# Gathers without a bound for their indices, in a transformer block with two edge stages

## What is computed

```python
# GNN, for each of 4 heads
e = e_src[:, src] + e_dst[:, dst]
e = jnp.where(e > 0, e, NEG_SLOPE * e)
m = jax.ops.segment_max(e_h, dst, num_segments=N)
ex = jnp.exp(e_h - m[dst])
den = jax.ops.segment_sum(ex, dst, num_segments=N)
alpha = ex / jnp.maximum(den[dst], 1e-16)
out = jax.ops.segment_sum(alpha[:, None] * z_h[src], dst, num_segments=N)
...
# FFN, the routing over its own edges, then the experts
e = jax.nn.leaky_relu(a_src[src] + a_dst[dst], negative_slope=0.2)
msg = h[src] * alpha[:, :, None]
...
hh = jax.nn.gelu(x @ W1[ei] + b1[ei], approximate=False)
out = out + g[..., None] * (hh @ W2[ei] + b2[ei])
```

## Time and profile before

| | us |
|---|---|
| median of 3 runs | 3594.51 |
| lowest and highest | 3592.44, 3606.05 |
| span of the profiled execution | 3619.3 |
| POOL busy in it | 2173.4 |
| DVE busy in it | 1738.3 |
| PE busy in it | 1464.3 |
| ACT busy in it | 1386.9 |

### The profile page before, as it was taken

One profiled execution on the slowest core, in us unless ns is written; L12 is line 12 of the kernel. 1 busy time (PEld: TensorE's weight loads), 2 busy tenths in 40 slices (PEclk: granted clock), 3 DMA queues, 4 the chain that ended last, 5 costly groups with the idle time before them and its releaser, 6 DMA issues. The chain is left out here.

```text
span 3619.3 us, 23786 instructions
## 1 busy us (share of the span) xinstructions
PE 1464.3 (40%) x4490; PEld 918.6 (25%) x4490; DVE 1738.3 (48%) x3400; ACT 1386.9 (38%) x3540; POOL 2173.4 (60%) x2136
## 2 busy tenths in 40 slices
PE   2556610211212112211514665656665656663014
PEld 1333410111111111111512333433343333332003
DVE  7667786877778777864922111111111111111137
ACT  1332346666776677752402222322222222221112
POOL 0543656666666666645666666666666666666750
PEclk8677855555555555555556777867787777776557
DMA  3421645565666656636521111111111111111166
GB/s 127 130 63 53 170 130 178 199 197 183 199 199 207 192 184 203 196 113 197 149 86 17 33 36 33 38 21 36 36 36 35 33 24 36 35 35 36 17 203 234
DMA packets 227607, 391.61 MB, mean 108 GB/s; under 512 B 53316, under 2 KB 184051, under 8 KB 220113
## 3 DMA queue, kind: packets, MB, share of 16 engines
q1 hardware_dynamic: 137556, 258.07, 20.5%
q0 software_dynamic: 80880, 124.27, 14.9%
q10 hardware_dynamic: 9100, 8.50, 0.7%
HBM read 201.15 MB, written 189.55 MB: 108 GB/s over the span
## 5 line engine op out<-in xcount | busy, mean ns | idle before, releaser
L1229 POOL DMA_INDIRECT stage_got<-ffn_rows,stage_idx x1024 | 1033.8, 1010 | 546.1 <-issue 326.6
L1229 POOL DMA_INDIRECT edges_got<-gnn_rows,edges_idx x728 | 727.9, 1000 | 354.3 <-issue 310.6
L1340 DVE TENSOR_TENSOR_SCAN stage_y<-stage_decays,stage_y 128x960 f32<-128x960 f32 (+2 forms) x288 | 527.1, 1878 | 172.8 <-ACT stage_y L1348 94.9
L2151 PE MATMUL stage_ph<-ffn_xt_all,stage_w 128*128 (+1 forms) x896 | 428.4, 618 | 284.0 <-ACT stage_hid L2205 78.7
L1363 ACT ACTIVATE stage_rows<-stage_y 128x896 f32<-128x896 f32 x224 | 372.5, 1816 | 7.7 <-issue 7.7
L2233 DVE TENSOR_TENSOR search_found<-stage_po,stage_b 128x256 f32<-128x256 f32 x196 | 75.9, 420 | 579.8 <-DMA x_again_X<-in_x_dram 425.3
L1637 PE MATMUL stage_pm<-setup_ident,stage_mix_parts 128*128 128x128 f32 x98 | 32.4, 434 | 778.7 <-ACT stage_mix_parts L1663 634.5
L1327 ACT ACTIVATE stage_y<-edges_got,stage_y 128x64 f32<-128x64 f32 x784 | 230.9, 393 | 244.2 <-issue 200.9
L2163 PE MATMUL stage_po<-stage_w,stage_start_parts 128*128 128x256 f32 x784 | 243.6, 437 | 189.9 <-issue 153.6
L2151 PEld LDWEIGHTS stage_ph<-ffn_xt_all,stage_w 128*128 128x128 f32 x896 | 190.6, 218 | 468.9 <-issue 372.6
L2163 PE MATMUL stage_po<-stage_w,stage_hid 128*128 128x256 f32 x784 | 237.6, 426 | 164.7 <-issue 162.4
(11 more groups left out here) (473 smaller groups left out, 2871.8 us busy)
## 6 DMA issues: line engine op xcount, KB each, us to landing
state_gnn<-stage_rows SPq DMA_DIRECT2D x56, 1848.0 KB
y<-search_found SPq DMA_DIRECT2D x28, 896.0 KB
tail_fin_y<-y SPq DMA_DIRECT2D x7, 3584.0 KB
stage_got<-ffn_rows,stage_idx POOLq DMA_INDIRECT x1024
edges_got<-gnn_rows,edges_idx POOLq DMA_INDIRECT x784
state_ffn<-stage_rows SPq DMA_DIRECT2D x64, 192.0 KB
mix_rows<-stage_mix_parts SPq DMA_DIRECT2D x49, 131.0 KB
x_again_mix<-mix_rows SPq DMA_DIRECT2D x7, 917.0 KB
```

What stands on the lines that cost most here:

```text
L1229: pool.indirect_dma_start(out=got[:, u, t, :], out_offset=None, in_=self.row_dram[g.name][:, :], in_offset=bass.IndirectOffsetOnAxis(ap=id ...
L1340: ins = dve.tensor_tensor_scan(some, r[s][:, 0:b - a, :].rearrange("p c t -> p (c t)"), some, 0.0, ALU.mult, ALU.add)
L2151: mm = pe.matmul(ph[:, n % 4, 0:HALF], w1[:, e, k, f * P:(f + 1) * P], xt_all[:, k, bass.ds(b * (B * P) + half * HALF, HALF)], start=(k == ...
```

## The change

The indirect DMAs of `pool_gather`, 728 of the GNN and the FFN's 1024, are issued without `bounds_check` and without `oob_is_err=False`, which then has its default, true. The register with `NPAD - 1` is no longer loaded ahead of the two loops. Every other instruction stays, in its place; one line fewer in the file moves the numbers of the lines behind 1231 down by one. The gathers of line 1164 and all other indirect DMAs are as before.

```diff
                 for t in range(T):
                     pool.indirect_dma_start(
                         out=got[:, u, t, :], out_offset=None, in_=self.row_dram[g.name][:, :],
-                        in_offset=bass.IndirectOffsetOnAxis(ap=idx[:, u, t:t + 1], axis=0),
-                        bounds_check=bound, oob_is_err=False).then_inc(gathered[u], 16)
+                        in_offset=bass.IndirectOffsetOnAxis(ap=idx[:, u, t:t + 1], axis=0)).then_inc(gathered[u], 16)
```

## The result

The changed kernel takes 3623.35 us (median of 4 runs, 3620.16 to 3632.17) where the kernel before takes 3593.48 (4 runs, 3591.66 to 3606.05) beside it. The ratio is 1.0077 with a 95% interval of 1.0057 to 1.0097: 28 us slower, where 94 us faster was forecast.

The account below looks back on a forecast made before the run. The prediction took POOL, busy 2173 of 3619 us mostly with gathers, as the bound. FFN 69.6 us and GNN 24.8 us sum to 94.4, taking 3594.5 to 3500 us; the 8-in-10 range was 3340 to 3625.

Parts of the forecast that it names:

- The price of a bound: On POOL, each gather of line 1229 gets 0.068 us shorter without its bound; upper end 0.198 us.
- a bound that costs nothing seen: Rival: gathers on POOL stay at 0.997 us, pitch 1.30, time 3594 us; chance 0.30.
- a dearer way without one: Rival: each of the 1752 gathers grows by 0.068 us without a bound, 119 us, 3714 us; chance 0.15.
- the step follows POOL's row one for one: FFN loop: each step shortens by what its gathers lose, 1024 x 0.068 = 69.6 us; step 50.0 to 47.8 us.
- second rival: Shorter gathers, but both loops go at another engine's pace; only unbroken FFN stretches gain, 10 us, 3585 us; chance 0.08.
- held while POOL is gathering: FFN loop: matmuls and gelus get along slowly during POOL's gathers; last gelu starts 3.9 to 4.6 us after the row.
- The GNN's half: GNN loop: POOL at 89% and coupled to ACT, so half the saving counts, 728 x 0.068 / 2 = 24.8 us.
- room on PE: FFN loop: PE busy 708 of 1149 us, leaving room for a shorter step down to about 31 us of matmuls.
- POOL as the bound of the last chunks: FFN's last chunks, no matmul beside them: POOL alone is the bound, 65 gathers at 1.314 us each.

Follow-up runs that it names:

- e5: Kernel before with every second gather of the FFN's chunks left out (output is another): 2897.18 us, ratio 0.8064.
- e8: Kernel after with the experts' matmuls cut to one of two in the first layer, one of four in the second: 3510.02 us, ratio 0.9762.
- e7: Kernel before with the experts' matmuls cut to one of two in the first layer, one of four in the second: 3485.89 us, ratio 0.9696.
- e11: Kernel after with one already met wait behind every gather of both loops: 3654.22 us, ratio 1.0139.
- e12: Kernel after with two already met waits behind every gather of both loops: 3692.91 us, ratio 1.0257.
- e1: Kernel before with the bound taken off in the GNN's 728 gathers only: 3630.03 us, ratio 1.0069.
- e6: Kernel before with every second gather of the GNN's chunks left out from the fifth chunk on: 3379.15 us, ratio 0.9388.
- e2: Kernel before with the bound taken off in the FFN's 1024 gathers only: 3623.15 us, ratio 1.0048.
- e17: Kernel after with one drain behind each chunk of the GNN alone: 3593.48 us, ratio 1.0014.
- e9: Kernel before with one drain on POOL behind the last gather of each FFN chunk: 3567.74 us, ratio 0.9896.

## Why the prediction was wrong

**The price of a bound** was right in kind: 0.068 us taken, 0.050 measured, with the controls on lines 1164 and 2334 at 1056 and 1000 ns. The rival of a bound that costs nothing seen, and that of a dearer way without one, fall by the same rows. The 1280 ns that the prediction estimated for a branch on each of 128 indices, and set aside, are 25 times the measured 50. The page of the Trainium skill that I brought in for the first of them (Perfetto Trace Analysis, DMA Instruction — SWDGE) is not contradicted: the gather's end moved by 0.050 us with the check gone, so the check isn't hidden beside something slower.

**The step that failed** is "the step follows POOL's row one for one". It predicted 47.8 us; the FFN's step has a median of 50.1 before and 50.2 after, and POOL's wait grew by what its row lost, which is what the prediction had named as the mark of its second rival. Half of the observation under it was sound: e5 shows how strongly the gathers hold PE, 22 us of the step. But the last gelu isn't let go by the row's end: it started 3.9 to 4.6 us behind a row of 32 before, and starts 5.3 to 6.2 us behind most of them now. The row's last gather in a step of the kernel after, and the last three gelus (the last of them starts near 2492.4):

```profile
2485.32 0.95 POOL L1229 DMA_INDIRECT stage_got<-ffn_rows,stage_idx  x1 [0.30 <-issue]
2491.27 1.68 ACT L2204 ACTIVATE stage_start_parts<-stage_ph,stage_b 128x448 f32<-128x448 f32 x3 [19.02 <-DMA x_again_X<-in_x_dram]
```

The gelus kept their place in the step while the row before them ended 1.6 us earlier. The inference was the mistake. I read "held while POOL is gathering" as a hold in proportion to the row's length. The runs show a hold that is there with long unbroken rows (428 us of spells), all but gone with half the gathers (2 us) and gone with the row broken after 16 (none, step 47.8 us), where a shorter gather then pays 24 us. The same gathers closer together don't lessen it: PE's spells went from 428 to 501 us, and in e8 POOL's stops come after 64 gathers where e7's come after 96. That the closeness itself does this is argued from these pairs; the run that was to space the gathers failed to. The e5 row can't be seen in a trace of before; but the earlier trace rows with PE busy 708 us of 1149, and 14.82 us of waiting for a gelu in the earlier trace rows, should have made me ask what PE itself did in between. Its starts on a grid of 0.70 us were in the trace.

**The GNN's half**, 24.8 us of gain, is a loss of 9 us between the two traces, and of some 18 over all of them (17 without e11 and e12, which have waits added). In the profiled executions without a break in the GNN, the loop takes 1047 to 1063 us with the bound (seven) and 1069 to 1079 without (six). ACT's spells became fewer there, not more (315 to 197 us), so they are not what lengthens it. What goes with the missing bound in every trace is POOL's wait for ACT's copies between 495 and 1550: 7 to 34 us in those seven, 67 to 112 in those six. What makes ACT's copies late isn't settled, so for the larger part of the measured loss the cause stays open. The term failed in its sign: a shorter row of gathers gave the GNN nothing, not half of its length.

**The second rival** came nearest in mechanism and was wrong in price: it had nothing to set against its 10 us of gain. No case of mine had the sign right for the right reason: I had looked for a loss only in longer gathers. Loops of the FFN without a break take 1576 to 1588 us with the bound and no added waits (before, e1, e6), 1584 to 1602 without (after, e2, e17): some 11 us more; with the GNN's 18 that makes up the measured 28 to 30 us. The range held the time, at 2 us from its upper end, but on account of the wrong case: that was luck.

**What was never in doubt**: room on PE (27.9 us by e5, 31 estimated), and POOL as the bound of the last chunks, where the pitch fell from 1.31 to 1.26 us as forecast.

## What to carry to other kernels

A busy engine with few waits isn't yet the bound: ask what its work does to the others, and test it by leaving half of that work out before pricing a saving in it. Where software-made gathers run in long rows beside matmuls or many small instructions, look for starts on a fixed grid (here 0.70 us) on the other engines; if they are there, break the row (here one drain per 16 gathers of the FFN, 1.0% faster), and only then shorten the gathers (2.2% with both in the FFN, but 0.9% when the GNN's gathers lose their bound too and keep their unbroken rows). A saving that only packs the same requests closer can cost time.

## What the runs showed of the hardware

- A bound in an indirect gather of 128 rows costs 0.050 us of 0.997; the gap of 0.30 us between gathers stays. With a drain behind every gather it is 0.058 us a gather of the FFN's loop and 0.123 of the GNN's.
- A drain behind a gather costs 2 us at every gather, and leaves 3.1 us idle in place of 0.3 at the end of an FFN chunk, 3.7 to 5.3 us on average at the end of a GNN chunk.
- Instruction starts on PE fall on multiples of 0.70 us some 16 gathers into an unbroken row of the FFN, until some 2 us after it; those on ACT some 21 gathers into one of the GNN, until 3.2 us after it. Two waits already met behind each gather don't move POOL's gathers (1.30 us apart) but lengthen PE's spells by 47% (428 to 629 us).
- PE's granted clock is 0.99 in e5's FFN loop, its upper level, where PE is busy 592 of 650 us. It averages 0.75 in the kernel before, and 0.79 in e9, which has no spells either but waits for POOL; so the spells alone don't decide it.

What the gathers fill isn't known. It isn't the DMA engines' bandwidth: their share is 0.16 in the FFN's window, where the spells are, and 0.24 in e5's, where they are not. It hangs on POOL's waits as well as its gathers. The runs on record come with spans and granted clocks, so they were recorded, which leaves the recording itself as a candidate: the Trainium skill, NOTIFIC — the notification-queue block, Overflow: three behaviours, one of which stalls the engine, says that the block's inner pipeline holds its producers back rather than lose a record. No run here shows a kernel without recording, and e11's spells grew with no instruction more in its trace, so that stays open.
